# Decoder block on one core: the context load at the head of SyncE's step

## The reference

```
x = x + self_attention(layernorm(x))           # causal, with ALiBi bias
x = x + cross_attention(layernorm(x), ctx)     # 120 keys and values from the context
x = x + tanh(layernorm(x) @ W @ A1 @ A2 + bias)
```

## Time and profile before

| | us |
|---|---|
| three executions | 2781.45, 2784.67, 2797.6 |
| their median | 2784.67 |
| the profiled execution | 2791.88 |
| its span | 2790.1 |
| TensorE busy in the span | 2495.2 |
| VectorE busy | 1714.9 |
| ScalarE busy | 1403.3 |
| granted TensorE clock, mean | 0.954 of full speed |

### The profile page before, as it was taken

The page is one execution under the profiler, slowest core; times in us unless marked ns, Lnnn a source line. Parts: engine busy times, 40 slices in busy tenths (PEclk is TensorE's granted clock), DMA queues, the critical chain, the costliest instruction groups (busy, mean ns, idle before and its releaser), DMA issues.

```text
span 2790.1 us, 70718 instructions
## 1 busy us (share of the span) xinstructions
PE 2495.2 (89%) x23737; PEld 2048.2 (73%) x23864; DVE 1714.9 (61%) x3714; ACT 1403.3 (50%) x3067; POOL 714.5 (26%) x1359
## 2 busy tenths in 40 slices
PE   3789999999999999999999999999999999999985
PEld 2577777777777777777777777777777777777774
DVE  3365666665666666666666566666666666656652
ACT  2245555555555545555555555555455555455542
POOL 2112222222222222222222222222222222222221
PEclk8799999999999999999999999999999999999996
DMA  3466556566556556556656655655665665665541
GB/s 74 63 89 90 88 88 96 84 90 93 82 85 96 91 83 96 84 87 96 90 83 93 92 87 87 96 89 85 96 88 81 93 95 85 92 87 87 90 76 21
DMA packets 162889, 240.65 MB, mean 86 GB/s; under 512 B 21790, under 2 KB 86030, under 8 KB 159766
## 3 DMA queue, kind: packets, MB, share of 16 engines
q1 hardware_dynamic: 161304, 239.99, 57.2%
q10 hardware_dynamic: 1536, 0.01, 0.0%
HBM read 53.12 MB, written 33.55 MB: 31 GB/s over the span
## 4 chain that ended last, share of the span: by engine, by line
PE 57%; DMA 24%; DVE 6%; SPq 4%; issue 4%; ACT 4%; ACTq 1%; POOL 0%; DVEq 0%; POOLq 0%
DMA q_stack<-q_nat 12%; PE ps_misc L474 10%; DMA ctx_in<-in_ctx 9%; PE ps_misc L488 9%; PE ps_max L540 4%; SPq L394 4%; PE ps_score L585 3%; PE ps_score L572 3%; PE ps_max L553 3%; PE ps_attend L600 3%; PE ps_max L530 3%; PE ps_score L574 3%; PE ps_score L576 3%; PE ps_misc L630 2%; PE ps_max L536 2%
## 5 line engine op out<-in xcount | busy, mean ns | idle before, releaser
L901 DVE TENSOR_REDUCE neg_max_s<-ps_max 128x2 f32<-128x512 f32 (+1 forms) x768 | 483.1, 682 | 111.3 <-PE ps_max L530 73.0
L750 ACT ACTIVATE probs<-ps_score 128x384 f32<-128x384 f32 x1024 | 470.0, 492 | 141.3 <-PE ps_score L576 135.4
L757 ACT ACTIVATE xprobs<-ps_score 120x512 f32<-120x512 f32 x512 | 295.5, 599 | 244.4 <-PE ps_score L585 237.1
L1018 POOL TENSOR_SCALAR ve_LN<-mv_LN 128x2 f32<-128x2 f32 x192 | 36.8, 191 | 1342.7 <-DVE mv_LN L923 1342.7
L574 PE MATMUL ps_score<-q_stack,k_stack 97*128 97x256 f32 x1024 | 378.1, 369 | 0.0
L909 DVE TENSOR_REDUCE neg_max_x<-ps_max 128x4 f32<-128x480 f32 x512 | 314.2, 651 | 70.3 <-PE ps_max L553 70.3
L572 PE MATMUL ps_score<-mask_k,ident_b 128*128 128x256 bf16 x1024 | 290.9, 284 | 22.6 <-DMA q_stack<-neg_max_t_s 15.0
L576 PE MATMUL ps_score<-q_stack,k_stack 97*128 97x256 f32 x1024 | 291.1, 284 | 0.0
L1044 POOL TENSOR_TENSOR res<-res,chain_n 128x512 f32<-128x512 f32 x64 | 82.4, 1288 | 605.2 <-ACT chain_n L795 605.2
L585 PE MATMUL ps_score<-xq_stack,xk_stack 97*120 97x256 f32 x1024 | 227.2, 314 | 3.5 <-DMA xq_stack<-neg_max_t_x 2.8
L574 PEld LDWEIGHTS ps_score<-q_stack,k_stack 97*128 97x128 f32 x1024 | 206.6, 202 | 1.5
(11 more groups left out here) (153 smaller groups left out, 6026.9 us busy)
## 6 DMA issues: line engine op xcount, KB each, us to landing
k_stack<-k_nat SPq DMA_DIRECT2D x192, 256.0 KB, 6.9
q_stack<-q_nat SPq DMA_DIRECT2D x192, 256.0 KB, 7.2
xq_stack<-q_nat SPq DMA_DIRECT2D x192, 256.0 KB, 6.0
xk_stack<-scr_xk SPq DMA_DIRECT2D x192, 128.0 KB, 3.7
x_in<-in_x SPq DMA_DIRECT2D x64, 256.0 KB, 3.2
scr_xk<-k_nat SPq DMA_DIRECT2D x32, 512.0 KB, 6.8
out_y<-res SPq DMA_DIRECT2D x64, 256.0 KB, 2.2
ctx_in<-in_ctx SPq DMA_DIRECT2D x32, 240.0 KB, 7.9
```

The costliest lines, as they stand in the source:

```text
L750: act.activation(probs[:, h % 8, :], bank_of("SCORE", i, b, h)[:, P:4 * P], ACT.Exp)\
L757: act.activation(xprobs[0:C, at:at + 2, :], blocks(bank_of("XSCORE", i, b, u))[0:C], ACT.Exp).then_inc(sem("xprobs_ready"), 1)
L901: dve.tensor_reduce(o, ins, AX.X, ALU.max, negate=True).then_inc(sem("max_taken"), 1)
```

## The change

In SyncE's list the entry `LOAD_CTX` moves from behind `XQ_STACK` to the head of the step. It keeps its offset, its wait and its transfer.

```
 ORDER = {
     "SP": (
-        ("STORE", -3, 0), ("XMAX_STACK", -2, 0), ("LOAD_X", 1, 0), ("XK_STACK", -1, 0),
-        ("MAX_STACK", 0, 0), ("XQ_STACK", -1, 0), ("LOAD_CTX", 0, 0),
+        ("LOAD_CTX", 0, 0), ("STORE", -3, 0), ("XMAX_STACK", -2, 0), ("LOAD_X", 1, 0), ("XK_STACK", -1, 0),
+        ("MAX_STACK", 0, 0), ("XQ_STACK", -1, 0), 
         ("K_STACK", 1, 0), ("Q_STACK", 1, 0), ("XK_SAVE", 0, 0),
```

## The result

The changed kernel takes 2876.11 us (median of four executions, 2874.47 to 2877.47) against 2787.74 us for the kernel before in the same comparison: 1.0309 times, with a 95% interval of 1.0286 to 1.0333. It is slower by 3.1%, and lies 26 us above the upper end of the range forecast (2850 us).

The account below looks back on a forecast made before the run. TensorE, busy 89%, was taken as the bound, with only idle time and slow clock to give back. Per pair -0.8 + 1.44 = +0.6, counted as +0.2 on the mean; 31 x 0.2 = +6, giving 2791 us, range 2738 to 2850 us.

Parts of the forecast that it names:

- What is late next: Keys' restack lands at 1266.5, holding ScalarE's write of the cross keys; TensorE stands idle 3.6 us before score 13.
- The issue, the queries' restack, the store: SyncE's queue: moving the load costs its followers nothing; queries' restack slowed 0, store and cross maxima 0, at most 0.6 us.
- The gain of 0.8 us at score 13: TensorE: keys' restack lands 0.6 us earlier without the context ahead, so score 13 starts 0.8 us earlier than 1268.67.
- That the loss of the clock was covered before: Short pair, context's transposes: the 1.44 us half-clock loss is almost all covered by the wait for the exponential, costing 0.3 us.
- The clock: TensorE behind score 13: the clock falls after the moved stall, costing 1.44 us uncovered, bounds 0 and 3.09 us.
- The third rival: Clock stays low for long: 6.84 us low stretch in most pairs, 50 to 71 us slower, up to 2856 us; chance 0.18.

Follow-up runs that it names:

- the filled kernel before: Kernel before, plus 13 matmuls computing nothing needed ahead of the context's transposes, where TensorE was idle for 2.9 us: 2775.46 us, 0.9964 of the kernel before.
- the one with filled maxima: Changed kernel plus 8 matmuls computing nothing needed ahead of the maxima of every even sequence, where TensorE waits for `q_stack`: 2809.03 us, 1.0073 of the kernel before.

## Why the prediction was wrong

*What is late next* held. The wait of 2.93 us was not removed but moved: forecast 3.6 us idle before score 13, measured 3.40; ScalarE's wait forecast above 100 us and about 4 us each, measured 158.9 and 4.89; the third copy 7.6 us, measured 7.59. The run with a tile of its own shows that this wait is the cause of the stall, and that without it the kernel is faster than before.

*The issue, the queries' restack, the store* held: 10.25 against 10.18 us. The wait for `q_stack` is 2.5 us a time against 2.3, and the run with the load elsewhere loses as much. The store and the cross maxima's stacks cost nothing that shows.

*The gain of 0.8 us at score 13* held: 82.03 before and 81.06 after, each with the clock kept, 1.0 us.

*That the loss of the clock was covered before* held: the filled kernel before keeps its 82.03 us. The text priced it at 0.3 us in a short pair, and it was 0.

*The clock* is the step that failed, in the sum for a pair: "-0.8 + 1.44 = +0.6, giving 82.6 us", taken as +0.2 on the mean. It assumed the short fall of the kernel before at the new place, and no more at the other one than before. Measured is -1.0 from the order, then 4.3 us of clock in every pair against 0.7 in the mean before: -1.0 + 4.3 - 0.7 = +2.6 a pair. (This closes by its making: the terms are differences of the same four lengths of a pair.) Two terms were too small. The stretch behind score 13 is 6.84 us long, not 3.4; its bound of 3.09 us was right (2.99 by the busy time, 2.8 in the length of the pair) and the value taken from it was not. And the fall behind the wait for `q_stack` comes in every pair, at 1.5 us; the text left it in the share of the long pairs, without a term. It stood in the trace of the kernel before, in the long pairs:

```profile
1390.03:1405.03 15.00, 12.91 (x126) 10.77 (x125) 9.00 (x18) 4.57 (x10) 1.29 (x1) 0.89 0.65 80
```

Those 15 us hold the wait for `q_stack`; 0.89 is 3.3 us at half clock, in a long pair of which the text priced only the first stretch of 6.84 us. At the price measured above, that fall is 1.5 of the 3 us by which long pairs were longer; the longer first stretch is left with the other half.

The third rival had this mechanism, with 85.0 us a pair and 2856 us at most, at a chance of 0.18. Its top was 20 us under the result, and the range ended below even that. The range should have reached the case where each pair pays both falls. What made its chance small was that long pairs were one in four before. That number belonged to the old stall, and the change replaced that stall by a longer one at another place.

The Trainium skill, "TensorE: Matmul & The Clock Gate", section "HAM oscillation", describes a fall of the clock paid in every iteration, and the pairs of this kernel agree in kind. Its price, throttled time x (1 - 1.2/2.4), gives an estimate of 5.1 us for 3.4 + 6.84 us at half clock. Measured are 4.3 us. TensorE was idle for 0.86 us of it, 0.4 us by that price; the other 0.4 us is split about evenly between the two falls (1.5 us measured against 1.7 by the busy time, 2.8 against 2.99), and what covers it was not resolved.

Still open: why the changed kernel settles in the pair with both falls. The run with more work and the one with filled maxima show that the moment at which the clock falls within a stall matters beside its length; they do not say which shift would let it out.

## What to carry to other kernels

Before a wait is taken away, look for the wait that ends at the same moment: here a small row, 24.5 us in 18 waits, became 158.9 us, and only the removal of both gave the 4.5%. A stall has two prices, its idle time and what the clock takes behind it, and the second depends on where it stands and what covers it. If a wait cannot go, its order can: asking for the same landing a few entries later cost no memory and brought as much as a separate tile.

## What the runs showed of the hardware that was not expected

Matmuls that compute nothing made the kernel faster: 15 ahead of one stall gained 103 us of 2876, and 7 gained about as much (102 us, medians of separate comparisons). Idle times of about 2 us passed with no fall in some pairs and with one in others of the same kernel (77.6 and 79.1 us, mostly in turn), while 3.4 us were followed by a fall each time in the pairs examined.

Two stalls of 3.4 us at the same place of one kernel (the one with filled maxima) were followed by 6.84 us at half clock in one pair and by 3.41 us in another. In the first the clock fell 0.9 us before work resumed, in the second after it had.

The length of a pair can repeat closely: 85.3 to 85.4 us in 26 pairs of the changed kernel, the same with 0.65 us of work added, and the same with the load of the context at another place in the queue.
